# Two layouts of the split query and key rows in memory, on one Trainium2 core

## The chip, the core and the metric

The kernel runs on one core of one Trainium2 chip. The metric is the device time of one execution in microseconds (us); lower is better. The engines are TensorE (PE; its weight loads are PEld), VectorE (DVE), ScalarE (ACT), GpSimd (POOL) and SyncE (SP), which issues nearly all transfers (DMAs). The core's DMA engines, 16 of them, carry the transfers.

## The reference

Two layers, each an attention over a context and an attention with a feed-forward part, on x of 16 sequences of 256 tokens with 256 features. What matters here are the two many-headed self-attentions: layer 0 has 32 heads of width 8, layer 1 has 16 heads of width 16.

```python
x = x + L0_xattn(ctx, ctx, layernorm(x))            # part A
# part B: layer 0, width 8
q = (xn @ wq).reshape(B, S, 32, 8); k, v likewise
att = einsum('bqhd,bkhd->bhqk', q, k) / sqrt(8)
o = einsum('bhqk,bkhd->bqhd', softmax(att), v).reshape(B, S, D) @ wo + x
# then one of 8 expert feed-forwards, by position
x = x + L1_xattn(layernorm(x), ctx)                 # part C
# part D: layer 1, width 16
q = ((h @ wq + bq) * 16 ** -0.5).reshape(b, s, 16, 16); k, v likewise
scores = einsum('bqhd,bkhd->bhqk', q, k)
o = einsum('bhqk,bkhd->bqhd', softmax(scores), v).reshape(b, s, d) @ wo + bo
# then a mixture of 8 experts with 2 per token, capacity a quarter of the tokens
```

## The kernel before

**Two stages.** `layers` works through the 16 sequences; `experts` then does the last mixture of experts for all tokens. The change lies in `layers`.

**Pipeline of rounds.** Round r works on several sequences at once: part A and the projections of B for sequence r+1 and part D's end for r-2 (thread "Q", `lin1`), the scores, exponentials and value products of the width-16 heads of r-2 and then of the width-8 heads of r (threads "S", "T", "E", "V"), and the end of B, part C and the projections of D for r-1 (thread "P", `lin2`). Every engine walks the same string `ORDER`, whose letters say which thread takes its next step. Rounds -1 to 1 and 14 to 17 are written out; rounds 2 to 13 are a hardware loop of two rounds per pass.

**Why rows go to memory.** The score product of a head has only 8 or 16 features to contract over. The kernel splits each fp32 value of q and k into a high part (fp32r) and the rest, and stacks three parts of the head's features on the partitions, so that one product with 32 rows (width 8) or 64 rows (width 16) gives q_high k_high + q_high k_low + q_low k_high. The four or two heads of a "slot" fill the 128 partitions. The high part is made by ACT (L1247, L1251 for width 8, L1303 for width 16), the rest by DVE (`rest`, L945, L947). The tiles are qTQ/PRQ (k high, k rest) and pTQ/cTQ (q high, q rest) for width 8, and PRP/pTP and cTP/cxTP for width 16. The q side has its high part twice and the rest once, and so has the k side, in another order.

**The way through memory.** SP puts the parts into the DRAM tensors k8, q8, k16, q16 (in the profile `k_dram` and `q_dram`) with `put` (L356), one transfer for each of the three parts and each half c of the features: 6 for k, 6 for q, 12 for each stack, 128 KB each. Then `fetch` (L362) loads the stack: KS and QS, each in two halves of 512 KB. A fetch waits until all parts of its half have landed (`s_parts`, 16 per transfer, threshold `PARTED`). The first score product of the width-16 heads waits for the first halves of KS and QS (`s_stack`, in `scores`).

**Spare rows.** Per head 8 (width 8) or 16 (width 16) rows are left. On the k side they hold 1.0 and on the q side 0.0, put there once at the start (`spare_rows`). Two of them per head carry the negated row maximum, high part and rest: DVE writes them into columns `h.spare` and `h.spare + 1` of MT (L964, L966), TensorE transposes MT (L642), and DVE adds the result to QS (L978), so that the second product of K with this sum (L662) gives the shifted scores, to which ACT applies exp (L1184). The value products (L677) follow.

**Order on SP around the change.** All of this is one queue in program order. In a round: the k puts of width 8, the k puts of width 16, the q puts of width 16, the fetch of the width-16 stack, then the q puts and the fetch of the width-8 stack. Each step begins with a wait for the ACT or DVE instruction that makes the part.

Of the kernel before, what the change touches and what calls it, by code (L numbers as in the profile page):

```python
# [22 lines left out]
ALU = mybir.AluOpType  # L23
# [3 lines left out]
P = 128  # L27
EPS = 1e-5
SLOT = 32
PARTS = 3  # L30
# [7 lines left out]
def now(eng, value):  # L38

    eng.compute_val(value)  # L40
    return value
# [9 lines left out]
class Events:  # L51
# [4 lines left out]
    def __init__(self, sem, names):  # L56
        self.sem, self.names, self.done = sem, names.split(), []
# [17 lines left out]
class Heads:  # L75


    def __init__(self, name, width, D, sem):
        self.width = width
        self.nh = SLOT // width  # L80
        self.slots = D // SLOT
        self.pairs = self.nh // 2
        self.heads = D // width
        self.groups = self.heads // 4
        self.rows = P // self.nh
        self.spare = PARTS * width
        self.scale = float(width) ** -0.5
        self.scored = sem(f"{name}_scored")
        self.maxed = sem(f"{name}_maxed")
        self.negated = sem(f"{name}_negated")  # L90
        self.parted = sem(f"{name}_parted")
        self.turned = sem(f"{name}_turned")
        self.shifted = sem(f"{name}_shifted")
        self.st = sem(f"{name}_st")
        self.exp = sem(f"{name}_exp")
        self.pv = sem(f"{name}_pv")
        self.os = sem(f"{name}_os")
# [45 lines left out]
def layers(nc, a, out, scratch, sem, ident, ones, cst, logits, bank):  # L143
    B, S, D = a["x"].shape
    NE, _, FD = a["L0_ffn_w1"].shape
    DC, FC = D // P, FD // P
    assert S == 2 * P and DC == 2 and FC == 8 and B % NE == 0 and B % 2 == 0
# [8 lines left out]
    with ExitStack() as stack:  # L156
# [31 lines left out]
        PARTED_OF = {8: {"k": (KHQ, KLQ), "q": (QHQ, QLQ)}, 16: {"k": (KHP, KLP), "q": (QHP, QLP)}}  # L188
# [22 lines left out]
        vecs, b1rows = OS[8][0:24, 0, 0:P], OS[8][:, 1, 0:P]  # L211


        PART_RESTS = {"k": (False, False, True), "q": (False, True, False)}

        def part_rows(width, w, part, c):

            h = heads_of[width]
            rows_d = scratch[f"{w}{width}"].rearrange("(c h x) t -> c h x t", c=DC, x=h.rows)
            return rows_d[c, :, part * width:(part + 1) * width, :], PARTED_OF[width][w][PART_RESTS[w][part]][:, c, :]  # L220

        def spare_rows(width, w):

            h = heads_of[width]
            return scratch[f"{w}{width}"].rearrange("(h x) t -> h x t", x=h.rows)[:, h.spare:, :]

        def stack_half(width, w, c):

# [11 lines left out]
        def halves(b):  # L240
            return bank[b][:, :].rearrange("p (c t) -> p c t", c=2)
# [15 lines left out]
        s_parts = {(s, w, c): sem(f"s_parts_{w}{s}{c}") for s in (8, 16) for w in "kq" for c in range(DC)}  # L257
        s_stack = {(s, c): sem(f"s_stack_{s}{c}") for s in (8, 16) for c in range(DC)}
        s_spare = sem("s_spare")
        PARTED, STACKED = 16 * PARTS, 16 * 2  # L260
        h0, h1 = Heads("h0", 8, D, sem), Heads("h1", 16, D, sem)
        heads_of = {8: h0, 16: h1}

# [51 lines left out]
        def _(sp):  # L315
# [6 lines left out]
            def load_w(b):  # L322
                e = now(sp, b % NE)
                sp.dma_start(W1[:, :, :], w1_d[e]).then_inc(s_w, 16)
                sp.dma_start(W2[:, :, :], w2_d[e]).then_inc(s_w, 16)
                sp.dma_start(B2[:, 0, :], a["L0_ffn_b2"][e].partition_broadcast(P)).then_inc(s_w, 16)
# [12 lines left out]
            for dst, src in rest_loads:  # L339
                sp.dma_start(dst, src).then_inc(s_rest, 16)  # L340
            sp.wait_ge(s_cst, 2)
            for width, h in heads_of.items():
                for w, filled in (("k", QM[:, 0, :].bitcast(F32)), ("q", MT[8][:, 0, :, :].rearrange("p r x -> p (r x)"))):
                    sp.dma_start(spare_rows(width, w), filled[0:h.heads, :].unsqueeze(1).broadcast_to([h.heads, h.rows - h.spare, D])).then_inc(s_spare, 16)
            sp.wait_ge(s_spare, 16 * 4)
            load_w(0)
            load_cx(CXC, 0, s_cxC)
            sp.sem_inc(s_store, 16)

            def put(width, w, rest):  # L350

                for part_ in range(PARTS):
                    if PART_RESTS[w][part_] == rest:
                        for c in range(DC):
                            dst, src = part_rows(width, w, part_, c)
                            sp.dma_start(dst, src).then_inc(s_parts[width, w, c], 16)  # L356

            def fetch(width, b, c):

# [10 lines left out]
            def lin1(b, e, par, a_, d_):  # L370
# [24 lines left out]
                if a_:  # L395
                    fetched(8, b)
                    made(act, "B1", b, "kh")
                    put(8, "k", False)
                    made(dve, "B1", b, "kl")
                    put(8, "k", True)  # L400
                yield
                if a_:
                    made(act, "B1", b, "qh")
                    put(8, "q", False)
                    made(dve, "B1", b, "ql")
                    put(8, "q", True)
# [481 lines left out]
        def _(v):  # L888
# [61 lines left out]
            def maxima(h, b):  # L950

                base = {n: now(v, b * k) for n, k in dict(head=h.heads, slot=h.slots).items()}
                for slot, p in product_of(range(h.slots), range(h.pairs)):
                    for u in range(2):
                        j = 2 * p + u
                        v.wait_ge(h.scored, base["head"] + (slot * h.nh + j + 1))
                        v.tensor_reduce(MX[:, slot % 2, j, :], halves(u), AX, ALU.max, negate=True).then_inc(h.maxed, 1)  # L957
                    if p == h.pairs - 1:
                        low = MX[:, slot % 2, 0:h.nh, :].rearrange("p j r -> p r j")
                        parts = MT[h.width][:, slot % 2, :, :].rearrange("p r (j x) -> p r j x", x=h.rows)  # L960
                        v.wait_ge(h.maxed, base["head"] + (slot + 1) * h.nh)
                        if slot >= 2:
                            v.wait_ge(h.turned, base["slot"] + (slot - 1))
                        v.tensor_copy(parts[:, :, :, h.spare].bitcast(F32R), low).then_inc(h.negated, 1)  # L964
                        v.wait_ge(h.negated, base["slot"] + (slot + 1))
                        v.tensor_tensor(parts[:, :, :, h.spare + 1], low, parts[:, :, :, h.spare], ALU.subtract).then_inc(h.parted, 1)  # L966
                    yield

            def shifts(h, b, prev):
# [11 lines left out]
            def threads(r, par, b_, p_, a_, d_):  # L981
                hd, hb = lined_up(r, b_, d_)
                return {"S": chain(maxima(h1, r - 2) if hd else idle(8), maxima(h0, r) if hb else idle(16)),
                        "T": chain(shifts(h1, r - 2, hd[1]) if hd else idle(8), shifts(h0, r, hb[1]) if hb else idle(8)),
                        "E": idle(N_EXP), "V": idle(N_VALUE),
                        "P": lin2(r - 1, 1 - par) if p_ else idle(N_LIN2), "Q": lin1(r + 1, r - 2, par, a_, d_)}
# [711 lines left out]
def program(nc, a, out):  # L1698
    B, S, D = a["x"].shape
    T, NE = B * S, a["L1_ffn_w1"].shape[0]  # L1700
    CAP = -(-T // 4)
    scratch = {n: nc.dram_tensor(f"{n}_dram", shape, F32, kind="Internal").ap()
               for n, shape in (("tokens", (T, D)), ("slots", (NE * CAP, ROW)), *((f"{w}{width}", (4 * D, D)) for w in "kq" for width in (8, 16)))}
    with ExitStack() as stack:
        def sem(name):
            return stack.enter_context(nc.semaphore(name))

        cst_t = stack.enter_context(nc.sbuf_tensor("cst", [P, C_ALL], F32))
        ones_t = stack.enter_context(nc.sbuf_tensor("ones", [P, P], F32))
        logits = stack.enter_context(nc.sbuf_tensor("logits", [P, T // P, NE], F32))  # L1710
        bank = [stack.enter_context(nc.psum_tensor(f"bank{i}", [P, 512], F32)) for i in range(8)]
        ident, ones = cst_t[:, C_IDENT:C_IDENT + P], ones_t[:, :]
        layers(nc, a, out, scratch, sem, ident, ones_t, cst_t, logits, bank)
        experts(nc, a, out, scratch, sem, ident, ones, cst_t, logits, bank)
# [46 lines left out]
```

## Time and profile before

| what | value |
|---|---|
| three runs | 2344.63, 2328.07, 2341.23 us, median 2341.23 |
| the profiled execution | 2332.09 us, of it the span 2330.3 |
| PE matmul busy | 1990.7 us, 85% |
| DVE busy | 1356.4 us, 58% |
| ACT busy | 1049.8 us, 45% |
| POOL busy | 500.4 us, 21% |
| `layers` ends, `experts` begins | at about 1808 us |
| a round in the middle | 101 to 103 us |
| SP's transfers (queue q1) | 211280 packets, 226.58 MB, 30.9% of 16 engines |

The page of the profile has six parts: busy time of each engine, the same in 40 slices, the DMA queues, the chain that ended last, the costliest groups of instructions, and the transfers by issuing line. In the slices PE is at 90% or more from the fourth to the last round of the middle; its clock share is 9 of 10 there. The chain that ended last lies in `experts` for the most part and says nothing on the stage that is changed; for that stage the waits and the timeline are to be read.

### The profile page before, as it was taken

How to read it: one execution, taken by the hardware profiler on the slowest of the kernel's cores; microseconds unless marked ns; L12 is line 12 of the kernel's file. 1: busy time of each engine (PE TensorE's matmuls, PEld its weight loads, DVE VectorE, ACT ScalarE, POOL GpSimd, SP SyncE). 2: the span in 40 equal slices, each digit the busy share in tenths (PEclk: the TensorE clock that was granted, in tenths of full speed). 3: DMA queues.
4: the chain of work that ended last, by engine and by line, in shares of the span. 5: the costliest groups of instructions: out<-in, count | busy, mean ns of one | idle time of the engine just before them, and what ended most of it. 6: DMA issues, size and time to landing. Idle time of an engine off the chain costs nothing. (4 is left out here: it accounts for less than half of the span.)

```text
span 2330.3 us, 42953 instructions
## 1 busy us (share of the span) xinstructions
PE 1990.7 (85%) x13779; PEld 1480.5 (64%) x13779; DVE 1356.4 (58%) x3560; ACT 1049.8 (45%) x2004; POOL 500.4 (21%) x413
## 2 busy tenths in 40 slices
PE   5689999999999999999999999989865007999997
PEld 4456666676666667666666766666553007999996
DVE  2345666675666667566666756656523505676664
ACT  0244556465555646555564655556422003333332
POOL 1102121220212122121212212120120271322222
PEclk8689999999999999999999999999986558999998
DMA  5222352524335241433525243251211444434333
GB/s 164 73 72 77 106 167 69 156 67 136 96 104 162 75 155 67 136 97 103 163 73 155 67 136 100 90 161 66 87 35 63 158 134 125 87 78 120 78 83 71
DMA packets 223826, 245.30 MB, mean 105 GB/s; under 512 B 13098, under 2 KB 214763, under 8 KB 223616
## 3 DMA queue, kind: packets, MB, share of 16 engines
q1 hardware_dynamic: 211280, 226.58, 30.9%
q0 software_dynamic: 12336, 16.10, 4.0%
q8 instruction: 110, 1.80, 0.3%
q14 instruction: 100, 0.82, 0.1%
HBM read 158.24 MB, written 85.33 MB: 105 GB/s over the span
## 5 line engine op out<-in xcount | busy, mean ns | idle before, releaser
L957 DVE TENSOR_REDUCE MX<-bank 128x2 f32<-128x512 f32 x768 | 493.5, 684 | 267.0 <-PE bank L625 265.8
L1184 ACT ACTIVATE PT<-bank 128x512 f32<-128x512 f32 x768 | 416.7, 596 | 217.8 <-PE bank L662 215.2
L625 PE MATMUL bank<-KS,QS 32*128 32x256 f32 (+1 forms) x1536 | 206.5, 349 | 68.6 <-DMA QS<-q_dram 50.3
L625 PEld LDWEIGHTS bank<-KS,QS 32*128 32x128 f32 (+1 forms) x1536 | 123.6, 199 | 158.2 <-issue 80.4
L677 PE MATMUL bank<-PT,VA 128*32 128x256 f32 x3072 | 213.1, 396 | 11.7 <-ACT PT L1184 10.1
L662 PE MATMUL bank<-QM,KS 32*128 32x256 f32 (+1 forms) x1536 | 192.4, 328 | 12.3 <-ACT PT L1184 11.5
L1542 ACT ACTIVATE hid<-bank,b1T 128x512 f32<-128x512 f32 x128 | 87.9, 687 | 234.9 <-issue 188.8
L662 PEld LDWEIGHTS bank<-QM,KS 32*128 32x128 f32 (+1 forms) x1536 | 118.3, 189 | 110.4 <-issue 83.8
L1453 POOL DMA_INDIRECT out_dram<-yo,rows x64 | 107.1, 1674 | 290.8 <-DMA out_dram<-yo,rows 135.0
L477 POOL TENSOR_TENSOR rrB<-uwB,cst 128x4 f32<-128x4 f32 x16 | 16.3, 1017 | 610.2 <-DVE uwB L932 610.2
L1509 PE MATMUL bank<-W2h,hTh 128*128 128x256 f32 x512 | 145.4, 284 | 0.0
L1509 PE MATMUL bank<-W2h,hTl 128*128 128x256 f32 x512 | 144.1, 282 | 0.0
L1509 PE MATMUL bank<-W2l,hTh 128*128 128x256 f32 x512 | 143.9, 281 | 0.0
L677 PEld LDWEIGHTS bank<-PT,VA 128*32 128x32 f32 x3072 | 82.5, 111 | 92.6 <-issue 35.0
L1196 ACT ACTIVATE OS<-bank 128x256 f32<-128x256 f32 x192 | 73.8, 384 | 141.6 <-PE bank L677 141.3
L828 PE MATMUL bank<-W,HT 128*128 128x256 f32 x512 | 125.4, 388 | 0.0
L978 DVE TENSOR_TENSOR QM<-QS,bank 128x256 fp32r<-128x256 f32 x256 | 106.4, 416 | 32.5 <-PE bank L642 32.2
L576 PE MATMUL bank<-qTP,W 128*128 128x256 f32 x512 | 124.5, 386 | 0.0
L642 PE MATMUL bank<-cst,MT 128*128 128x128 f32 x512 | 111.5, 301 | 5.3 <-DVE QM L978 2.7
L1477 PE MATMUL bank<-cst,xg 128*128 128x128 f32 x136 | 18.5, 282 | 110.6 <-DMA xg<-slots_dram 110.6
L828 PEld LDWEIGHTS bank<-W,HT 128*128 128x128 f32 x512 | 92.3, 190 | 20.3 <-issue 6.2
L576 PEld LDWEIGHTS bank<-qTP,W 128*128 128x128 f32 x512 | 92.2, 190 | 18.6 <-issue 6.2
(277 smaller groups left out, 3890.2 us busy)
## 6 DMA issues: line engine op xcount, KB each, us to landing
W<-in_L_ffn_w_dram SPq DMA_DIRECT2D x54, 1024.0 KB, 7.4
KS<-k_dram SPq DMA_DIRECT2D x64, 512.0 KB, 5.3
QS<-q_dram SPq DMA_DIRECT2D x64, 512.0 KB, 5.8
xg<-slots_dram SPq DMA_DIRECT2D x18, 520.0 KB
slots_dram<-zeros SPq DMA_DIRECT2D x16, 520.0 KB, 4.0
k_dram<-qTQ SPq DMA_DIRECT2D x64, 128.0 KB, 2.4
q_dram<-pTQ SPq DMA_DIRECT2D x64, 128.0 KB, 5.4
k_dram<-PRP SPq DMA_DIRECT2D x64, 128.0 KB
```

The costliest lines, as they stand in the source:

```text
L576: i = mm(halves(b)[:, o, :], lhsT[:, c, o * P:(o + 1) * P], rhs[:, c, :], start=c == 0, stop=last and c == 1)
L625: x = mm(halves(u)[:, r, :], Q[strip, slot, r * P:(r + 1) * P], K[strip, slot, :], start=True, stop=True)
L642: x = t.transpose(bank[4][:, D + r * P:D + (r + 1) * P], MT[h.width][:, slot % 2, r, :], ident)
L662: x = mm(halves(2 + u)[:, kc, :], K[strip, slot, kc * P:(kc + 1) * P], QM[strip, slot % 2, :], start=True, stop=True)
L677: x = mm(bank[4][SLOT * j:SLOT * (j + 1), 0:D], V[:, kc, n * per:n * per + SLOT], PT[:, n % 8, kc, :], start=kc == 0, stop=kc == 1, tile_p ...
L828: x = mm(halves(7)[:, r, :], HT[:, f, r * P:(r + 1) * P], W2[:, f, :], start=f == 0, stop=f == FC - 1)
L957: v.tensor_reduce(MX[:, slot % 2, j, :], halves(u), AX, ALU.max, negate=True).then_inc(h.maxed, 1)
L978: v.tensor_tensor(QM[:, slot % 2, :], QS[h.width][:, slot, :].bitcast(F32), bank[4][:, D:2 * D], ALU.add).then_inc(h.shifted, 1)
L1184: s_.activation(PT[:, n % 8, :, :], halves(2 + n % 2), ACT.Exp, scale=h.scale).then_inc(h.exp, 1)
L1453: g.indirect_dma_start(out=out, out_offset=bass.IndirectOffsetOnAxis(ap=rows_[j % 2][:, r:r + 1], axis=0), in_=yo[j % 2][:, r, :], in_offs ...
L1509: x = mm(bank[YB[r]][:, 0:D], hT[p][:, f, r * P:(r + 1) * P], W2S[i][q][:, f, :], start=(n, f) == (0, 0), stop=(n, f) == (len(TERMS) - 1, ...
L1542: s_.activation(hid[:, f % 4, :], bank[HB[f % 4]][:, :], ACT.Relu, bias=b1T[:, bass.ds(e, 1), f]).then_inc(s_hid, 1)
```

## The change

The rows of a stack are ordered by feature and not by part. Each feature has four rows next to each other in memory: its three parts and one spare. The two equal parts of a feature are neighbours (k: parts 0 and 1, q: now parts 1 and 2, since q's rest moves to part 0), so that one transfer with a repeated source writes both. A stack takes 8 puts in place of 12. The spare rows are now one per feature: 8 transfers at the start in place of 4, and MT's columns are 3 and 7 of each head. The bytes written and the fetches stay as they are, and so do all instructions of the other engines.

```diff
-        self.spare = PARTS * width
+        self.spare = PARTS
...
-        PART_RESTS = {"k": (False, False, True), "q": (False, True, False)}
-
-        def part_rows(width, w, part, c):
-
-            h = heads_of[width]
-            rows_d = scratch[f"{w}{width}"].rearrange("(c h x) t -> c h x t", c=DC, x=h.rows)
-            return rows_d[c, :, part * width:(part + 1) * width, :], PARTED_OF[width][w][PART_RESTS[w][part]][:, c, :]
-
-        def spare_rows(width, w):
-
-            h = heads_of[width]
-            return scratch[f"{w}{width}"].rearrange("(h x) t -> h x t", x=h.rows)[:, h.spare:, :]
+        PART_RESTS = {"k": (False, False, True), "q": (True, False, False)}
+        SPARE = PARTS
+
+        def stack_rows(w, width):
+
+            return scratch[f"{w}{width}"].rearrange("(c p x) t -> c p x t", c=DC, p=P)
+
+        def part_rows(w, width, rest, c):
+
+            at = [i for i in range(PARTS) if PART_RESTS[w][i] == rest]
+            dst = stack_rows(w, width)[c, :, at[0]:at[-1] + 1, :]
+            return dst, PARTED_OF[width][w][rest][:, c, :].unsqueeze(1).broadcast_to([P, len(at), D])
+
+        def spare_rows(w, width, c):
+
+            return stack_rows(w, width)[c, :, SPARE, :]
...
-        PARTED, STACKED = 16 * PARTS, 16 * 2
+        PARTED, STACKED = 16 * 2, 16 * 2
...
-                    sp.dma_start(spare_rows(width, w), filled[0:h.heads, :].unsqueeze(1).broadcast_to([h.heads, h.rows - h.spare, D])).then_inc(s_spare, 16)
-            sp.wait_ge(s_spare, 16 * 4)
+                    for c in range(DC):
+                        sp.dma_start(spare_rows(w, width, c), filled).then_inc(s_spare, 16)
+            sp.wait_ge(s_spare, 16 * 4 * DC)
...
-                for part_ in range(PARTS):
-                    if PART_RESTS[w][part_] == rest:
-                        for c in range(DC):
-                            dst, src = part_rows(width, w, part_, c)
-                            sp.dma_start(dst, src).then_inc(s_parts[width, w, c], 16)
+                for c in range(DC):
+                    dst, src = part_rows(w, width, rest, c)
+                    sp.dma_start(dst, src).then_inc(s_parts[width, w, c], 16)
...
-                        v.tensor_tensor(parts[:, :, :, h.spare + 1], low, parts[:, :, :, h.spare], ALU.subtract).then_inc(h.parted, 1)
+                        v.tensor_tensor(parts[:, :, :, 2 * h.spare + 1], low, parts[:, :, :, h.spare], ALU.subtract).then_inc(h.parted, 1)
```

On SP, in the loop, from the puts of k's rest (width 16) to the first fetch, the rows before are these (the shape is that of the destination; `s_parts_k160` is the semaphore of the k parts, width 16, half 0):

```order
L356 DMA k_dram<-pTP 8x16x256 [waits dve_D1,s_cst]
L356 DMA k_dram<-pTP 8x16x256
L40 REGISTER_ALU
L356 DMA q_dram<-cTP 8x16x256 [waits act_D1,s_cst]
L356 DMA q_dram<-cTP 8x16x256 x3
L40 REGISTER_ALU
L356 DMA q_dram<-cxTP 8x16x256 [waits dve_D1,s_cst]
L356 DMA q_dram<-cxTP 8x16x256
L40 REGISTER_ALU
L40 ISA [waits h1_st,s_cst]
L362 DMA KS<-k_dram 128x4x256 [waits s_parts_k160,s_cst]
L362 DMA QS<-q_dram 128x4x256 [waits s_parts_q160,s_cst]
```

and in the changed kernel, at the same place:

```order
L359 DMA k_dram<-pTP 128x256 [waits dve_D1,s_cst]
L359 DMA k_dram<-pTP 128x256
L40 REGISTER_ALU
L359 DMA q_dram<-cTP 128x2x256 [waits act_D1,s_cst]
L359 DMA q_dram<-cTP 128x2x256
L40 REGISTER_ALU
L359 DMA q_dram<-cxTP 128x256 [waits dve_D1,s_cst]
L359 DMA q_dram<-cxTP 128x256
L40 REGISTER_ALU
L40 REGISTER_ALU [waits h1_st,s_cst]
L365 DMA KS<-k_dram 128x4x256 [waits s_parts_k160,s_cst]
L365 DMA QS<-q_dram 128x4x256 [waits s_parts_q160,s_cst]
```

The four puts of a high part are two of twice the size, no step has moved past another, and the leading size of every destination is 128, where it was 8 (here) or 16 (width 8).

On PE, at the turn from one round to the next inside the loop, the rows before are:

```order
L569 MATMUL bank<-cst,CXA 128x128 x3
L700 MATMUL bank<-cst,OS 128x128 [waits h0_os,dve_D1]
L700 MATMUL bank<-cst,OS 128x128 x3
L625 MATMUL bank<-KS,QS 128x256 [waits h0_maxed,s_stack_160]
L625 MATMUL bank<-KS,QS 128x256 x3
```

and in the changed kernel:

```order
L572 MATMUL bank<-cst,CXA 128x128 x3
L703 MATMUL bank<-cst,OS 128x128 [waits h0_os,dve_D1]
L703 MATMUL bank<-cst,OS 128x128 x3
L628 MATMUL bank<-KS,QS 128x256 [waits h0_maxed,s_stack_160]
L628 MATMUL bank<-KS,QS 128x256 x3
```

Nothing has moved here but the line numbers; the fourth row is where PE asks for the first halves of the width-16 stack.

## Rows read from the trace of the kernel before

**Rows 1.** Page, part 5 (line, engine, operation, tiles | busy, mean ns | idle before, releaser).

```profile
L625 PE MATMUL bank<-KS,QS 32*128 32x256 f32 (+1 forms) x1536 | 206.5, 349 | 68.6 <-DMA QS<-q_dram 50.3
```

**Rows 2.** PE's waits, 60 to 1790 us (total us, times, longest us).

```profile
PE bank L625 <- DMA QS<-q_dram: 50.3, 13, 12.2
```

**Rows 3.** Timeline of PE at turns of rounds (start, us, what [idle before <-releaser]).

```profile
241.02 0.50 PE L625 MATMUL bank<-KS,QS 64*128 64x256 f32 x4 [3.61 <-DMA QS<-q_dram]
...
337.93 0.60 PE L700 MATMUL bank<-cst,OS 128*128 128x128 f32 x4
342.08 0.80 PE L625 MATMUL bank<-KS,QS 64*128 64x256 f32 x4 [3.56 <-DMA QS<-q_dram]
...
442.78 0.67 PE L569 MATMUL bank<-cst,CXA 128*128 128x128 f32 x4 [3.77 <-issue]
...
1566.27 0.80 PE L625 MATMUL bank<-KS,QS 64*128 64x256 f32 x4 [4.48 <-DMA QS<-q_dram]
...
1660.85 0.80 PE L625 MATMUL bank<-KS,QS 64*128 64x256 f32 x4 [4.74 <-DMA QS<-q_dram]
...
1756.07 0.80 PE L625 MATMUL bank<-KS,QS 64*128 64x256 f32 x4 [12.18 <-DMA QS<-q_dram]
```

**Rows 4.** Timeline of SP before the turn at 338 us (duration over all x).

```profile
322.56 2.51 SPq L356 DMA_DIRECT2D k_dram<-qTQ  x4
...
326.80 2.49 SPq L356 DMA_DIRECT2D k_dram<-PRP  x4
...
330.84 2.42 SPq L356 DMA_DIRECT2D q_dram<-cTP  x4
333.44 1.26 SPq L356 DMA_DIRECT2D q_dram<-cxTP  x2
335.01 0.40 SPq L362 DMA_DIRECT2D KS<-k_dram  x1
337.56 0.38 SPq L362 DMA_DIRECT2D QS<-q_dram  x1
```

**Rows 5.** Timeline of ACT and DVE: the makers of the width-16 parts.

```profile
324.42 0.84 ACT L1303 ACTIVATE PRP<-bank,cols 128x256 fp32r<-128x256 f32 x2 [0.95 <-PE bank L576]
...
328.20 0.84 ACT L1303 ACTIVATE cTP<-bank,cols 128x256 fp32r<-128x256 f32 x2 [0.84 <-PE bank L576]
...
329.07 0.88 DVE L945 SCALAR_TENSOR_TENSOR cxTP<-bank,cols,cTP 128x256 fp32r<-128x256 f32 x2 [1.30 <-ACT cTP L1303]
...
1649.52 0.88 DVE L945 SCALAR_TENSOR_TENSOR cxTP<-bank,cols,cTP 128x256 fp32r<-128x256 f32 x2 [1.29 <-ACT cTP L1303]
...
1742.90 0.88 DVE L945 SCALAR_TENSOR_TENSOR cxTP<-bank,cols,cTP 128x256 fp32r<-128x256 f32 x2 [1.06 <-ACT cTP L1303]
```

**Rows 6.** Stretches of 1 us: length, PE, PEld, DVE, ACT, POOL, PEclk, DMA share, GB/s.

```profile
324.00:325.00 1.00, 1.00 (x13) 0.47 (x15) 0.00 (x0) 0.58 (x2) 0.00 (x0) 1.00 0.76 212
...
331.00:332.00 1.00, 1.00 (x8) 0.82 (x5) 0.60 (x2) 0.80 (x2) 0.00 (x0) 1.00 0.56 170
...
344.00:345.00 1.00, 1.00 (x6) 0.67 (x6) 0.90 (x5) 0.00 (x0) 0.00 (x0) 0.50 1.10 380
```

**Rows 7.** Page, part 6: transfers by line (count, KB each, median us from issue to landing).

```profile
slots_dram<-zeros SPq DMA_DIRECT2D x16, 520.0 KB, 4.0
k_dram<-qTQ SPq DMA_DIRECT2D x64, 128.0 KB, 2.4
...
tokens_dram<-H SPq DMA_DIRECT2D x16, 256.0 KB, 2.7
```

**Rows 8.** Issue time on SP by tile (ns min/median/max, first and last start).

```profile
L389 SPq DMA_DIRECT2D tokens_dram<-H x16: 378/404/411, 313.6 to 1802.0; - x16
...
L392 SPq DMA_DIRECT2D slots_dram<-zeros x16: 585/626/672, 315.3 to 1803.7; - x16
```

**Rows 9.** Timeline of PE: the eighth score group after two turns.

```profile
261.19 0.51 PE L625 MATMUL bank<-KS,QS 64*128 64x256 f32 x4
...
546.24 0.79 PE L625 MATMUL bank<-KS,QS 64*128 64x256 f32 x4 [3.98 <-DMA QS<-q_dram]
...
567.35 0.51 PE L625 MATMUL bank<-KS,QS 64*128 64x256 f32 x4
```

More of the change, by code:

```diff
@@ L341, in _ @@
             sp.wait_ge(s_cst, 2)
-            for width, h in heads_of.items():
+            for width in heads_of:
                 for w, filled in (("k", QM[:, 0, :].bitcast(F32)), ("q", MT[8][:, 0, :, :].rearrange("p r x -> p (r x)"))):
-                    sp.dma_start(spare_rows(width, w), filled[0:h.heads, :].unsqueeze(1).broadcast_to([h.heads, h.rows - h.spare, D])).then_inc(s_spare, 16)
-            sp.wait_ge(s_spare, 16 * 4)
+                    for c in range(DC):
+                        sp.dma_start(spare_rows(w, width, c), filled).then_inc(s_spare, 16)
+            sp.wait_ge(s_spare, 16 * 4 * DC)
             load_w(0)
```

## The prediction

> **What bounds the kernel now.** I read the page's costliest groups first, then PE's waits, then the timelines around the largest of them. In the stage of layers PE is busy nearly throughout, so a transfer counts only where PE stands still for it. The score products of L625 do: PE was idle 68.6 us ahead of them, 50.3 of it until a QS stack had landed [rows 1]. These are 13 waits, the longest 12.2 us [rows 2]. The timeline puts eleven of them at turns of rounds, where the first width-16 score asks for the first halves of KS and QS [rows 3]. Nine, from 241.02 to 1566.27, are of one kind: the waits there are 3.6, 3.6, then others of this size, and 4.5 us. The tenth (1660.85) has 4.74 and the last (1756.07) 12.18. With about 0.6 us for the two small ones elsewhere, the nine hold 50.3 - 12.2 - 4.7 - 0.6 = 32.8 us. Five further turns are where the hardware loop jumps back; there PE is idle some 3.8 us in front of L569 with no releaser that the profile shows [rows 3], and the stack is there by the time PE asks. These five I leave as they are.
>
> What ends the wait at 342.08? Back along SP's queue [rows 4]: the QS fetch is issued at 337.56 and PE resumes 4.5 us later. Before that SP issues puts without a real pause from 322.56 to 334.70, each for about 0.6 us: 6 for k of width 8, 6 for k of width 16, 6 for q of width 16. The last q parts had been ready at 329.07 + 0.88 = 329.95 on DVE [rows 5], but their put starts at 333.44, 3.5 us later. The first one takes until 337.56 to land, 4.1 us, where a put of width 8 takes 2.4 at the median [rows 7]. So two delays stand between q's rest and the stack: SP's queue of issues (3.5 us), and slow landing (4.1 for 2.4 us).
>
> **The slow landing.** While the width-8 puts move, the DMA share is 0.76 at 212 GB/s; while the width-16 puts move it is 0.56 at 170 GB/s [rows 6], with the same 128 KB and the same issue pace. In the fetches behind it is full at 380 GB/s. The width-16 puts look as if about half of the DMA engines carried them, each full: 12 x 131 KB = 1.57 MB at 170 GB/s are 9.2 us, which is why they end at the landing at 337 and not with the issues. The Trainium skill has a rule for it (DMA: Bandwidth & Descriptors, "Why a DMA increments its semaphore by 16 and not by 1"): a transfer is spread over the largest number of engines up to 16 that divides the slowest dimension of both sides. By it 8x16x256 against 128 partitions runs on 8 engines, and 128x2x256 runs on 16. The trace agrees as far as the share goes. By the rule the pace doubles and the sum is the one below; by the row alone, should the pace stay, it is that of the first rival.
>
> **The parts of the change.**
> - Fewer issues: 8 puts for 12 in each stack. The nearest rows for the new shapes: a store of 128x2x256 is issued in 0.40 us, the repeated source of the zeros in 0.63 [rows 8]. A pair costs 0.40 to 0.63, a single put 0.40 to 0.60, so a stack 3.2 to 4.9 us for 7.3. I take 0.6 for the pair and 0.4 for the single. It turns out not to matter much, since SP then waits for data.
> - The new order of events at this turn: k of width 8 from 322.56, done by 325; k high of width 16 is made at 324.42 + 0.84 = 325.26 [rows 5], so its puts run from 325.3 to 326.5, the rest until 327.4. q high is made at 328.20 + 0.84 = 329.04: puts 329.1 to 330.3. q rest (329.95): first put at 330.4, where it was 333.44. It lands 2.4 us later [rows 7] plus 0.5, because 256 KB x 2 are ahead of it and at 380 GB/s take 1.4 us: 333.3. A 256 KB store lands in 2.7 us and a repeated source of 520 KB in 4.0 [rows 7]; neither asks for more. QS is issued at 333.4 and PE could go on 4.5 us later, at 337.9. PE has other work until 337.93 + 0.60 = 338.53 [rows 3, 5]. The wait is gone, with 0.6 us to spare. The distance from q's rest to PE's arrival is 8.6 us, the new chain 0.45 + 2.9 + 0.1 + 4.5 = 8.0. The order of PE's work is the same in every round, so I take all nine so: 32.8 us.
> - The tenth turn: q's rest is ready at 1649.52 + 0.88 = 1650.40, PE arrives at 1660.85 - 4.74 = 1656.11. The chain of 8.0 ends at 1658.4: 2.3 of the wait stay, 2.4 go.
> - The last turn: ready at 1743.78, PE idle from 1743.89 on. The chain ends at 1751.8 in place of 1756.07: 4.3 go.
> - The clock: after an idle turn the granted clock is at the lower of its two levels, 1.2 GHz, for some us (0.50 at 344 [rows 6]). From 241.02 to the eighth score group it took 20.17 us, from 546.24 to the eighth 21.11 [rows 3, 9]. The stretch is bound by DVE in part (0.90 busy at 344), so that a slow PE costs little. Half of this 0.94 at each of the eleven, 5 us, with bounds 0 and 10.
> - What costs nothing: the width-8 stack is fetched right behind, and its scores begin only after eight of width 16, some 23 us behind the turn; X, W and the contexts wait for other work and come a little earlier. The 8 spare transfers at the start carry the same 1 MB; they hold up only W and CXC, first needed far behind. Two DVE writes with another stride have the same element count. Were the cover of the width-8 stack gone, its chain would be the same 8 us.
>
> The sum: 32.8 + 2.4 + 4.3 + 5 = 44.5 us. Against the profiled execution's own 2332.1 that is 2287.6; it is 9 below the median of the three runs, which would give 2296.7. I predict the middle, 2292.
>
> **Rivals.**
> 1. *The pace of the width-16 puts stays.* Only issues are saved. k16 starts 1.5 us earlier (325.3 for 326.8), 1.57 MB at 170 GB/s and 1.5 us for start and receipt end at about 336, and the fetch ends near 340.3: 1.8 us of each of nine waits, 16 in all, nothing at the last two, where the puts start no earlier. That is 2316 to 2325. Against it speaks the drop of the share at the width-16 shape alone.
> 2. *Another wait takes the place.* PE comes to the next work 3.6 us earlier, and DVE, 0.90 busy behind the turn, or the second issue gap decides. Up to half is given back: 22 us less, 2310 to 2319. For it: DVE is nearly full there. Against it: DVE was itself idle in the wait, since its input is the awaited score.
> 3. *Slower.* The pairs and their scattered 2 KB pieces (each 4 KB apart, where a head's 8 or 16 rows were one run) land much later. The place is the landing between the puts and the QS fetch. It decides from the point where q's puts take more than 2.9 + 4.1 = 7.0 us to land, since 4.1 us lie between the new end of the chain, 337.9, and today's 342.0. At 10 us each of the eleven turns would lose 3: 2332 + 33 = 2365. The repeated source of 520 KB lands in 4.0 us [rows 7], far from it.
> 4. *It doesn't do what it says*: the waits are as long as before, by some release that I do not see; 2332 to 2341.
>
> **Chances.** The forecast 0.62, the first rival 0.13, the second 0.13, the third 0.07, the fourth 0.05. The range takes in the first two rivals in part and the bounds of the clock term: 2275 to 2320. What a measurement of this kernel can tell from no change is about 1%, 23 us. Faster by more: the forecast (0.62) and most of the second rival (0.1), with a piece of the first (0.03): 0.75. Within 1%: 0.18. Slower: 0.07.
>
> **What would show it.** In the changed trace the nine waits of L625 for QS should be gone or below 1 us, the tenth near 2.3 and the last near 8. The sum of QS waits of PE should fall from 50.3 to about 11. The DMA share during the width-16 puts should be above 0.7 or the puts come in short bursts. SP should show pauses between the put steps, where it had none, and the QS fetch should be issued about 3.5 us behind the DVE row of q's rest, where it was 7.6. The turns with the jump back should keep their idle time. I am wrong if the first put of q's rest takes over 3.5 us to land, if PE stops at the turn for DVE or for instructions instead, or if a pair is issued in more than 1 us.

## The result

The changed kernel takes 2299.77 us (median of 4 runs, 2296.69 to 2304.88); the kernel before, with one more run, 2336.81 (2328.07 to 2344.63). The ratio is 0.9848 with a 95% interval of 0.9824 to 0.9872: 37 us less between the medians, 36 by the ratio, where 45 were forecast. The profiled execution has a span of 2294.9 us, 35.4 less than that of before.

The waits of PE in the stage of layers (60 to 1790 us) in the changed kernel; columns are total us, times, longest us:

```profile
PE bank L572 <- issue: 31.5, 5, 6.9
PE bank L628 <- DVE MX L960: 25.1, 37, 3.2
...
PE bank L628 <- DMA QS<-q_dram: 11.7, 3, 9.2
```

The wait for the stack fell from 50.3 [rows 2] to 11.7 us. At the top now stands the wait of L572 (the old L569), the first product behind each of the five jumps back. PE's timeline at an ordinary turn, at the first jump, and at the last two turns:

```profile
325.31 0.60 PE L703 MATMUL bank<-cst,OS 128*128 128x128 f32 x4
325.90 0.50 PE L628 MATMUL bank<-KS,QS 64*128 64x256 f32 x4
...
428.92 1.11 PE L572 MATMUL bank<-cst,CXA 128*128 128x128 f32 x4 [6.83 <-issue]
...
1624.30 0.64 PE L628 MATMUL bank<-KS,QS 64*128 64x256 f32 x4 [2.27 <-DMA QS<-q_dram]
...
1719.09 0.80 PE L628 MATMUL bank<-KS,QS 64*128 64x256 f32 x4 [9.23 <-DMA QS<-q_dram]
```

The ordinary turn has no wait at all, where it had 3.56 us, and L628 takes 0.50 us and not 0.80, at full clock. The jump took 3.77 us before and takes 6.83 now [rows 3]. SP's queue before the same turn, and one stretch of the width-16 puts (length, PE, PEld, DVE, ACT, POOL, PEclk, DMA share, GB/s):

```profile
309.94 0.89 SPq L359 DMA_DIRECT2D k_dram<-qTQ  x2
...
312.71 0.88 SPq L359 DMA_DIRECT2D k_dram<-PRP  x2
313.78 0.84 SPq L359 DMA_DIRECT2D k_dram<-pTP  x2
316.50 0.88 SPq L359 DMA_DIRECT2D q_dram<-cTP  x2
317.55 0.87 SPq L359 DMA_DIRECT2D q_dram<-cxTP  x2
318.71 0.37 SPq L365 DMA_DIRECT2D KS<-k_dram  x1
321.74 0.37 SPq L365 DMA_DIRECT2D QS<-q_dram  x1
```

```profile
314.00:315.00 1.00, 1.00 (x7) 0.87 (x6) 0.93 (x4) 0.74 (x2) 0.00 (x0) 1.00 1.02 348
316.00:317.00 1.00, 1.00 (x8) 0.80 (x5) 0.55 (x2) 1.00 (x4) 0.00 (x0) 1.00 0.00 0
```

SP stands idle between the steps (314.6 to 316.5), and the puts of width 16 move at a DMA share of 1.02 and 348 GB/s, where they had 0.56 and 170 [rows 6]. The transfers in the changed kernel (count, KB each, median us to landing):

```profile
k_dram<-PRP SPq DMA_DIRECT2D x32, 256.0 KB, 2.4
...
k_dram<-pTP SPq DMA_DIRECT2D x32, 128.0 KB, 2.3
q_dram<-cxTP SPq DMA_DIRECT2D x32, 128.0 KB, 3.9
```

### The profile page after: what moved, and what is told of

It reads as the page before. It is cut to its first block and busy times, and to the rows that moved or that the text cites. A ratio compares the mean times of both kernels' runs of the same rounds, so it can differ in the third digit from the quotient of the medians.

```text
span 2294.9 us, 42817 instructions
## 1 busy us (share of the span) xinstructions
PE 1966.2 (86%) x13779; PEld 1461.5 (64%) x13779; DVE 1352.7 (59%) x3560; ACT 1049.8 (46%) x2004; POOL 500.0 (22%) x413
## 5 line engine op out<-in xcount | busy, mean ns | idle before, releaser
L628 PE MATMUL bank<-KS,QS 32*128 32x256 f32 (+1 forms) x1536 | 200.3, 340 | 38.0 <-DVE MX L960 25.1
L680 PE MATMUL bank<-PT,VA 128*32 128x256 f32 x3072 | 214.0, 398 | 11.7 <-ACT PT L1187 10.1
L628 PEld LDWEIGHTS bank<-KS,QS 32*128 32x128 f32 (+1 forms) x1536 | 119.3, 192 | 125.7 <-issue 71.8
L579 PEld LDWEIGHTS bank<-qTP,W 128*128 128x128 f32 x512 | 92.3, 190 | 18.5 <-issue 6.2
```

The lines of the kernel that those rows point to most:

```text
L579: i = mm(halves(b)[:, o, :], lhsT[:, c, o * P:(o + 1) * P], rhs[:, c, :], start=c == 0, stop=last and c == 1)
L628: x = mm(halves(u)[:, r, :], Q[strip, slot, r * P:(r + 1) * P], K[strip, slot, :], start=True, stop=True)
L680: x = mm(bank[4][SLOT * j:SLOT * (j + 1), 0:D], V[:, kc, n * per:n * per + SLOT], PT[:, n % 8, kc, :], start=kc == 0, stop=kc == 1, tile_p ...
```

## The experiments

Each is timed beside fresh runs of the kernel before. Their median was 2333.7 us for the first four experiments (the kernel before once more, the two widths, the single puts), 2335.6 for the holds and 2335.7 for the last two (the copy, the early KS). The ratios compare with these. "Changed kernel" means the one of the diff above, at 2299.8 us.

### The kernel before once more

> The kernel before once more, for its trace alone. It tells what of the difference between the two traces is there without any change. Ours: the nine waits of L625 for QS at turns (32.8 us) and the idle time at the five turns where the loop jumps back (19.4 us) come again within 2 us each; the first score product, which stood at 84.2 us before and at 79.8 us after the change, moves by some us from run to run, as the granted clock in the first 60 us does. Rival: the first score product stays at 84 us within 0.5, and the 4.4 us belong to the change of the spare rows' transfers.

Its span was 2327.6 us. The nine waits and the jumps came again: QS waits 49.7 us in 11, jumps 19.3 in five. The first score product stood here:

```profile
79.57 0.50 PE L625 MATMUL bank<-KS,QS 32*128 32x256 f32 x4
```

In the first trace of the same kernel it stood at 84.18 us, in that of the changed kernel at 79.75. So 4.4 of the 35.4 us between the two profiled executions are there without any change, and the rival, that they come from the spare rows' transfers, falls. In all the traces of this study it lies between 76.3 and 84.2 us.

### Width 16 alone, and width 8 alone

```diff
-        self.spare = PARTS
+        self.by_feature = width == 16
+        self.spare = PARTS if self.by_feature else PARTS * width
...
+                if not heads_of[width].by_feature:
+                    for part_ in range(PARTS):
+                        if OLD_RESTS[w][part_] == rest:
+                            for c in range(DC):
+                                dst, src = old_part_rows(width, w, part_, c)
+                                sp.dma_start(dst, src).then_inc(s_parts[width, w, c], 16)
+                    return
```

This is the main part of the edit for width 16 alone; the other has `width == 8` in the second line. `OLD_RESTS` and `old_part_rows` are the table and the function of the kernel before.

> The new layout and the paired puts for the stacks of width 16 alone; width 8 as before. Theory A (the puts of width 16 were slow since their leading size 8 put them on half of the DMA engines): nearly all of the gain is here, 2300 to 2305 us, QS waits of L625 at the nine turns near 0, DMA share in the width-16 puts well above 0.56. Theory B (the number of issues on SP decides, 12 for 8 per stack): half of the issues are saved, half of the gain, about 2318 us, waits of 1.5 to 2 us left at each of nine turns.

> The other half: paired puts for width 8 alone, width 16 as before (leading size 8). Theory A: the width-16 puts start 1.5 us earlier but move at 170 GB/s and a share of about 0.54, so 1.5 to 2 us of each of nine waits go and nothing at the last two turns: 2320 to 2325 us, QS waits in sum 33 to 37 us. Theory B: half of the gain, about 2318 us.

Width 16 alone: 2301.2 us, ratio 0.987 (0.9837 to 0.9903), the whole gain within the interval. Width 8 alone: 2327.6 us, ratio 0.9971 (0.9948 to 0.9994). PE's waits, first width 16 alone, then width 8 alone:

```profile
PE bank L598 <- issue: 31.1, 5, 6.6
...
PE bank L654 <- DMA QS<-q_dram: 11.8, 5, 7.7
```

```profile
PE bank L654 <- DMA QS<-q_dram: 37.7, 11, 12.1
PE bank L598 <- issue: 18.8, 5, 4.8
```

and a stretch of the width-16 puts in the second:

```profile
327.00:328.00 1.00, 1.00 (x6) 0.90 (x5) 1.00 (x3) 0.94 (x2) 0.00 (x0) 1.00 0.52 174
```

Both save the same number of issues. Width 8 alone comes out 3 us above what theory A gave, with waits of 1.8 to 3.7 us left at the nine turns. With the old shape 8x16x256 the share stays at 0.52 although the width-8 puts ahead of it are the new ones; with the leading size of 128 it is full. Theory A stands, theory B (half of the gain from either) falls. With the width-16 part alone, the cost at the jumps is there in full as well (31.1 us).

### The new layout with single puts

```diff
-        PARTED, STACKED = 16 * 2, 16 * 2
+        PARTED, STACKED = 16 * PARTS, 16 * 2
...
-                for c in range(DC):
-                    dst, src = part_rows(w, width, rest, c)
-                    sp.dma_start(dst, src).then_inc(s_parts[width, w, c], 16)
+                for part_ in range(PARTS):
+                    if PART_RESTS[w][part_] == rest:
+                        for c in range(DC):
+                            dst = stack_rows(w, width)[c, :, part_, :]
+                            sp.dma_start(dst, PARTED_OF[width][w][rest][:, c, :]).then_inc(s_parts[width, w, c], 16)
```

> The new layout, but one transfer for each part again: 12 for each stack, each with a leading size of 128. Theory A: like the changed kernel within 5 us (2300 to 2305), since the parts land fast and SP has pauses; waits at the nine turns below 1 us. Theory B: 12 issues take their time as before, 2315 to 2337 us. If a put of 128x256 is issued in 0.44 us as in the changed kernel and not in 0.6, theory B would have 2317.

2312.4 us, ratio 0.9917 (0.9889 to 0.9945): between the theories. PE's waits:

```profile
PE bank L574 <- issue: 33.3, 5, 7.0
...
PE bank L630 <- DMA QS<-q_dram: 18.5, 11, 8.6
```

Waits of 0.3 to 1.2 us are back at all nine turns. So with 12 issues the chain is a little too long, with 8 it just fits. At the turn at 335.81 the put of q's rest starts at 327.36, 1.1 us behind DVE (325.37 + 0.88), where the changed kernel has 0.2. Theory A fails here as I had put it (2300 to 2305): the leading size is not the whole of the gain, the number of issues counts too. By the ratios the layout alone brings 0.8% (19 us) and both together 1.5% (36 us). 7 us of the difference are the QS waits (18.5 against 11.7) and 2 the jumps; the remaining 8 are about what the two intervals leave open.

### What makes the jumps longer: three holds

The idle time at the five jumps rose from 19.4 to 31.5 us, which the prediction had not. DMA shares of 0.81 to 1.10 fill that stretch in the changed kernel. In the three experiments SP waits at different places of its queue until the first width-16 score pair of the next round is done:

```diff
+                    if c == 1:
+                        ready(h1.scored, b * h1.heads + 2)
                     fetch(16, b, c)
...
                 if a_:
+                    if not (isinstance(b, int) and b < 2):
+                        ready(h1.scored, (b - 2) * h1.heads + 2)
                     made(act, "B1", b, "qh")
```

The first piece is the full hold, ahead of the second halves of width 16. The second is the hold ahead of the width-8 q puts; the hold of the width-8 fetch is the same two lines one step later, ahead of that fetch. Each kernel has one of the three.

> The changed kernel, with one more wait on SP: the fetch of the width-8 stack (2 MB) is held until the first width-16 score pair of the next round is done. In the changed kernel the idle time of PE at the five jumps back rose from 19 to 31.5 us. Theory L: the code that PE fetches at the jump shares the DMA engines with stack traffic, and the more is in flight, the longer it takes (about 2.3 MB around the jump, 6 us at 380 GB/s). Without KS of width 8, issued 0.8 us behind the jump, some 0.5 MB less: 5 to 6 us for each jump, in sum 25 to 29, time 2293 to 2300 us. Rival M: the jump has a time of its own, set by PE's earlier arrival or by another engine's jump; the holds change nothing: 31 us and 2300 us.

> As the one before, but held already ahead of the width-8 q puts (0.77 MB), so that only the second halves of the width-16 stack (1 MB) are in flight around the jump. Theory L: 3.5 to 4.5 us for each jump, in sum 17 to 22, time 2285 to 2292 us; the width-8 stack still lands before its first score, 23 us behind the turn. Rival M: 31 us and 2300 us. A third way: the held transfers collide with something later, and the gain at the jumps is given back at the first width-8 scores or in the wait of ACT before part A's qTQ.

> Held already ahead of the second halves of the width-16 stack (and all that is behind them on SP), until the first width-16 score pair is done. At the jump nothing is in flight. Theory L: 1.5 to 3 us for each jump, in sum 8 to 15, time 2278 to 2288 us, if the second halves, landed some 6 us behind the first score, are there before the fifth score group 10 us behind it. Rival M: 31 us, and 2300 us or more.

The fetch of width 8 held: 2306.7 us (ratio 0.9857, 0.9822 to 0.9893), jumps 32.8 us. The width-8 puts held too: 2306.2 us (0.9858, 0.9827 to 0.9889), jumps 29.7 us. Neither differs from the changed kernel (0.9848), so up to here rival M holds. Everything behind the first halves held: 2280.2 us, ratio 0.9748 (0.9718 to 0.9779), 55 us below the kernel before and 20 below the changed one. Its waits of PE, its first jump, and the DMA share in the jump:

```profile
PE bank L574 <- issue: 15.3, 5, 3.4
...
PE bank L630 <- DMA QS<-q_dram: 10.5, 2, 7.6
```

```profile
433.00 0.65 PE L574 MATMUL bank<-cst,CXA 128*128 128x128 f32 x4 [2.80 <-issue]
```

```profile
431.00:432.00 1.00, 0.00 (x0) 0.00 (x0) 0.15 (x2) 0.00 (x0) 0.70 (x1) 1.00 0.02 8
```

In the changed kernel, at the same place:

```profile
425.00:426.00 1.00, 0.00 (x0) 0.00 (x0) 0.07 (x1) 0.00 (x0) 0.79 (x1) 1.00 1.04 352
```

With idle DMA engines the jump takes 2.8 to 3.4 us, and 15.3 in sum where full ones make it 31.5. It is below the kernel before (19.4), where stack traffic was in flight too. The two smaller holds show what hardly counts: the fetch of width 8, issued behind PE's stop, and the 0.77 MB of width-8 q puts, of which the first are issued 1.5 us ahead of it (420.57 in the changed kernel). My expectation for them (25 to 29 and 17 to 22 us at the jumps) was too low by 3.8 and 7.7 us at least. What counts is the 1 MB of second halves, issued 2.2 to 2.7 us ahead of PE's stop (SP's rows at 419.42 and 419.90; PE stops at 428.92 - 6.83 = 422.09).

The traces also show the code on its way. Beside SP's q1 the profile's list of DMA queues has two of kind "instruction": q8, with packets of 16 KB, and q14, with packets of 8 KB (columns: packets, MB, share of 16 engines). That q8 brings the code PE stands still for is read from the times. In the changed kernel no q8 packet starts from PE's stop (422.09) to 426.20; the first starts between 426.20 and 428.92, where PE resumes:

```profile
q1 hardware_dynamic: 1284, 1.27, 98.3%
q14 instruction: 1, 0.01, 0.5%
```

```profile
q1 hardware_dynamic: 988, 0.95, 102.0%
q8 instruction: 1, 0.02, 2.4%
```

In the full hold it starts within the first 0.20 us of the stop (430.20 to 430.40, nothing else starts there):

```profile
q8 instruction: 1, 0.02, 29.9%
```

At all five jumps of the full hold the q8 packet starts 0.1 to 0.2 us behind PE's stop. In the changed kernel it starts 4.2, 4.0, 1.4, 3.0 and 4.3 us behind it (jumps of 6.8, 6.8, 4.9, 6.1 and 6.9 us), in the first trace of before 0.7 to 1.5. From its start to PE's next product it is 2.6 to 3.4 us in all three. So the longer jump is a late start of this packet.

### Traffic of no use in their place

This kernel does extra work: a copy of 1 MB in each round that nothing reads.

```diff
                     if c == 1:
+                        if not first(b):
+                            ready(s_dum, b * 16)
+                        sp.dma_start(DUM, DUM_SRC).then_inc(s_dum, 16)
                         ready(h1.scored, b * h1.heads + 2)
```

> The kernel of the full hold, with traffic of no use put back where the second halves were: 1 MB copied from memory to memory in pieces of 1 KB, issued right behind QS's first half and ahead of the held transfers. SP's other transfers stay held. Theory L (bytes in flight at the jump make the code fetch late): each jump costs 5.5 to 7 us again, in sum 27 to 35 where the full hold had 15.3, and the time is 2292 to 2302 us. Rival: the hold helps by what it does to the order on SP or to the stack's own arrival, not by empty DMA engines: 15 us at the jumps and 2280 us.

2298.2 us, ratio 0.9849 (0.9818 to 0.9879), and the waits:

```profile
PE bank L581 <- issue: 27.6, 5, 5.8
...
PE bank L637 <- DMA QS<-q_dram: 10.8, 2, 8.5
```

The jumps cost 12.3 us more than without the copy, and the time is 18 us more by the medians, 24 by the ratios; the stack's own transfers are as in the full hold. So three quarters of the 16.2 us that the hold saved at the jumps come back with traffic alone, while the order of the stack's transfers stays held. The q8 packet starts 2.5 to 2.8 us behind PE's stop here. The traces give the difference without the start of the kernel: from the ordinary turn ahead of the first jump to the one behind the last it is 991.2 us in the full hold (333.89 to 1325.06), 1007.3 with the copy (329.81 to 1337.11) and 1012.4 in the changed kernel (325.90 to 1338.34). The 16.1 us between the first two exceed the idle time by 4; a part may be the clock, which stays at full after four of the five short jumps (the first product takes 0.65 us there, after each jump of the changed kernel 1.11).

### The hold in the kernel before

> The same hold in the kernel before (old layout, 12 puts). There PE's first scores wait for the first halves themselves: at the jumps they landed at about the time that the code had come. Theory L with the account of the turns: the jumps' idle time falls from 19 to 8 to 14 us, but as much comes back as a wait for QS at the same turns; the first halves land up to 1 us earlier at each of 15 turns, as no second halves share the engines with them. 2320 to 2334 us, that is 0 to 14 us below the kernel before. If instead the hold alone gave the gain, it would be near 2315.

The edit is the full hold, in the old layout. 2331.7 us, ratio 0.9975 (0.9958 to 0.9992), jumps 18.9 us, QS waits 48.4 us in 13. The hold alone is worth 4 us there. The expected fall at the jumps did not come: with the old layout the first halves themselves are in flight there, and this hold does not spare them. In its own trace PE stops at 434.97 - 3.77 = 431.20 and SP issues QS's first half at 431.31; the q8 packets start 0.8 to 1.3 us behind the stops. With the new layout under the full hold QS's first half is issued at 426.82, 3.4 us ahead of PE's stop at 430.20, and the engines are free by then. The two edits together give 55 us, singly 37 and 4.

### The first half of KS ahead of the q puts

```diff
                 put(16, "k", True)
+                if not first(b):
+                    ready(h1.st, b * h1.heads)
+                fetch_one(16, b, 0, "k")
                 yield
                 made(act, "D1", b, "qh")
...
-                    fetch(16, b, c)
+                    if c == 0:
+                        fetch_one(16, b, 0, "q")
+                    else:
+                        ready(h1.scored, b * h1.heads + 2)
+                        fetch(16, b, c)
```

`fetch_one` is one half of `fetch`: it waits for the parts of k or of q alone and issues that fetch. The lines are shown against the changed kernel.

> The kernel of the full hold, with the first half of KS (width 16) fetched ahead of the q puts, once the k parts have landed. Theory: the q rest's first put lands late (4.1 us for 2.3 of the k rest's) since the pairs ahead of it and the KS fetch behind it share the engines, and QS is queued behind KS. With KS moved into the pause of SP, QS lands 0.5 to 1.5 us earlier: the waits for QS at the last two turns, 2.9 and 7.6 us, fall by about that each, and the jumps' idle time (15.3 us) falls a little. 2274 to 2280 us. Rival: the wait of SP for the k parts delays the q puts by more than that; the last two waits get longer, 2281 to 2290.

2307.3 us, ratio 0.9894 (0.9869 to 0.9918), slower than the full hold by 27 us. It is slower, as the rival said, by more than it said, and not for the rival's reason. SP's queue:

```profile
320.78 0.37 SPq L370 DMA_DIRECT2D KS<-k_dram  x1
321.31 0.90 SPq L359 DMA_DIRECT2D q_dram<-cTP  x2
322.38 1.45 SPq L359 DMA_DIRECT2D q_dram<-cxTP  x2
328.37 0.37 SPq L370 DMA_DIRECT2D QS<-q_dram  x1
```

The wait for the k parts does not hold up the q puts: q's rest is ready at 321.07 + 0.88 = 321.95 and its put starts at 322.38. But from there to the QS fetch it is 6 us, where it was 4.2 in the changed kernel: the 512 KB of KS are now queued ahead. QS waits rose to 24.8 us in 11, jumps to 21.5, together 20.5 us more than in the full hold; the rest of the 27 is not accounted for.

## Why the prediction was right, and where it was not

**Which waits go.** The nine waits, 32.7 us, are gone (0.15 us are left at one), the tenth fell from 4.74 to 2.27, forecast 2.3. The last fell from 12.18 to 9.23, forecast about 7.9: 2.9 us for 4.3. The two small waits of the kernel before (0.44 and 0.21 us) stood behind two of the jumps, where the prediction had the stack there in time; they are gone too.

**The slow landing.** The first rival, that the pace of the width-16 puts stays, is out: the share went from 0.56 to 1.02, and width 16 alone, layout and pairs together, carries the gain. The rule of the Trainium skill that I set beside the row (DMA: Bandwidth & Descriptors, "Why a DMA increments its semaphore by 16 and not by 1") agrees with it: half the share and 174 GB/s with a slowest dimension of 8, the full share and 348 GB/s with 128.

**The chain.** At the ordinary turns it is longer than predicted. The put of q's rest starts 0.2 us behind DVE (317.55; forecast 0.45), lands after 4.1 us and not 2.9, and the fetch ends within 4.2 and not 4.5. Together that is up to 8.6 us, where I had 8.0, and PE arrives after 8.6. The spare time of 0.6 us is nearly used up: with single puts, which start q's rest 0.9 us later, the turn waits 0.98 us. That all nine waits went in full is thus partly luck. The landing is the mis-sized term, and by the prediction's own sign ("over 3.5 us to land") it had this step wrong: q's rest takes 3.9 to 4.1 us, where k's rest takes 2.3. The 512 KB ahead, which I priced at 0.5 us, do not explain it, since k's rest has the same 512 KB of pairs ahead. Nor does the KS fetch behind it alone: at the turn at 1532.54, with the same puts and the KS fetch as close, the QS fetch follows after 2.6 us (1524.39 to 1527.03). More bytes ahead do lengthen it (the early KS), but what makes the 4.1 in the loop stays open. At the last turn the put is not what is late: QS is issued 3.1 us behind it (1710.05 to 1713.11), as forecast, but its fetch takes 6.0 us (to 1719.09) and not 4.5. That is the missing 1.4 us; why is not shown.

**The issues.** A pair is issued in 0.43 us at the median and a single put too (0.44), less than I took for the pair, and as forecast it matters little, since SP waits for data: but see the single puts, where four more of them on each stack cost the margin.

**The clock.** The ten ordinary turns took 204.2 us from their first score to the eighth group, now 198.9: 5.3 us, forecast 5. No run separates the clock in it from the waits for DVE there.

**The jumps.** This is the step that failed: "These five I leave as they are". The same bytes are in flight in both kernels, but now earlier against PE's jump: at the first one the second halves are issued 2.2 to 2.7 us ahead of PE's stop, in the kernel before 1.1 to 2.6 us behind it. PE's code comes through the same engines, and its packet starts up to 4.3 us late. It costs 12.1 us, 2.4 for each jump. The full hold and the copy of no use show the cause: 15.3 us with empty engines, 27.6 with a copy of 1 MB.

**The sum.** 32.6 + 2.5 + 2.9 + 5.3 - 12.1 = 31.2 us, and the start 4.4 us earlier by chance: 35.6 for the 35.4 of the spans. The median, 2299.8, lies inside the range and 8 us above the forecast 2292; without the jumps it would have come out faster than forecast, by about 4.

**The other rivals.** Slower by late pairs: the 256 KB pairs land in 2.4 us and 2.6. Another wait in its place: DVE at L628 went from 17.2 to 25.1 us (in the second trace of before 17.4), so 8 us came in there. They lie in the stretch behind the turns, where PE at full clock meets DVE sooner, and the 5.3 us of the clock term are the net with them. The larger part given back, 12 us, went to the jumps, which this rival did not name.

**Open.** How the 16 engines' queues order code against data is not shown; only that 1 MB issued 2 to 3 us ahead of the jump delays the code packet, and what is issued from 1.5 us ahead of it on hardly does. What is left at an empty jump, 3 us each, was not tried. Why q's rest lands so late in the loop is open too.

## What to carry to other kernels

Look at the leading size of both sides of a transfer, not only at its bytes: 8x16x256 and 128x256 are the same 128 KB, but the first moved at about half of the DMA share. Where a wait in a hardware loop is shortened, look at what is then in flight when the loop jumps back; bytes needed ten microseconds later are best issued behind the jump. And where a chain has only half a microsecond to spare, price its landing from rows with the same neighbours in the queue: the same 128 KB took 2.3 us in one place of it and 3.9 to 4.1 in another.

## What the runs showed of the hardware

- A transfer with a leading size of 8 moved at a DMA share of 0.52 to 0.56 and 170 to 183 GB/s; with 128 at 1.02 and 348.
- A repeated source moves at the full pace: the pairs of 256 KB from 128 KB went at a DMA share of 1.02 and 348 GB/s and landed in 2.4 to 2.6 us at the median.
- A put of 128x256 was issued in 0.44 us, one of 16x8x256 or 8x16x256 in 0.58 to 0.60.
- The same put of 128x256 landed in 1.8 us at the median where all puts were single, and in 2.3 us in the changed kernel (k's rest); this is not explained.
- PE's jump back took 2.8 to 3.4 us with idle DMA engines and up to 7.0 with full ones; its 16 KB code packet started 0.1 to 0.2 us behind PE's stop in the first case and 1.4 to 4.3 us in the changed kernel.
- The first 80 us of the same kernel differ by up to 4.6 us between two executions; the granted clock from 20 to 60 us was 0.71 in one and 0.79 in the other.
